# The attention output kept as dimensions by tokens through DRAM, and its sums repeated by the load

## The chip, the core and the metric

The kernel runs on one core of one Trainium2 chip. The metric is the device time of one launch in microseconds (us), the median of several runs. The core has a matrix engine (PE, with its weight loads listed as PEld), a vector engine (DVE), a scalar engine (ACT), a general engine (POOL) and a queue engine (SP) that issues most DMA transfers. DRAM is the chip's large memory, SBUF the one on the core, and PSUM takes what PE writes.

## What is computed

The input x has 4 sequences of 1024 tokens with 256 features, all float32. Three layers follow each other: half a mixture-of-experts layer, attention, and half a mixture-of-experts layer again. The part at issue is the attention and what takes its result in:

```python
def _L0_attn_ref(x, W_dq, W_uq, W_dkv, W_uk, W_uv, W_o):
    ...
    scores = jnp.einsum('bqhd,bkhd->bhqk', Q, K) / math.sqrt(D_K)
    causal = jnp.tril(jnp.ones((Sx, Sx), dtype=bool))
    scores = jnp.where(causal, scores, -jnp.inf)
    attn = jax.nn.softmax(scores, axis=-1)
    out = jnp.einsum('bhqk,bkhd->bqhd', attn, V).reshape(Bx, Sx, N_HEADS * D_K)
    return out @ W_o
...
x = x + 0.5 * _L0_ffn_ref(_layernorm(x, axis=-1), ...)
x = x + _L0_attn_ref(_layernorm(x, axis=-1), ...)
x = x + 0.5 * _L0_ffn_ref(_layernorm(x, axis=-1), ...)
```

There are 16 heads of 16 dimensions, so the attention output of a token has 256 values, and it goes through the 256 by 256 out-projection `W_o`.

## The kernel before

The program is a row of phases, and each ends for all engines before the next begins. Names in the rows carry a short tag of the phase: `a` for the first mixture layer (`al` normalisation and gate scores, `ar` routing, `ae` experts), `q` for the query, key and value projections, `t` for attention, `b` for the second mixture layer (`bl`, `br`, `be`), `s` for the last sum. x stays in SBUF all along, tokens on the partitions, as 32 tiles of 128 tokens (`all_x`).

**Attention** (`phase_attention`) takes 16 groups, each of 4 heads of one sequence. The steps of groups 0 to 2 and 12 to 15 are written out, the nine between them are three passes of a loop over three steps. Step g holds three kinds of PE work, and `plan_step` sets their order by a table of costs:
- the row maxima of groups ahead (`score`, L1320, 48 units a group): PE fills one of three PSUM banks `psR`, DVE takes the maximum out (L1430, L1434). 37 units of the next group and 11 of the one behind it lie in a step, and a small transpose `turn_max` (L1326), whose result SP puts beside the queries by three small DMAs (L1276);
- transposed scores of its own group (`score_t`, L1339, with the causal mask added at L1342), 48 pieces through three banks `psS`, which ACT turns into exponentials (L1410);
- `pv` (L1353): values times exponentials, for 4 heads at once into `psO`, one bank for each half c of 512 query tokens. Rows 32h to 32h+16 of it are the 16 dimensions and, as the 17th, the sum of the exponentials of head h; columns are tokens.

ACT copies each finished `psO` into `oT` (L1398), half 0 some 5 us before half 1, which ends the group. In the next step PE transposes `oT` back to tokens by dimensions (`turn_out`, L1332, four 128 by 128 transposes for each half, at places 4 and 5 of the same three-bank ring), DVE copies the 17 useful columns of each head into `orow` (L1458), and SP stores that, one DMA a half (L1270), to `o_rows` in DRAM, tokens by 16 heads of 17 values. `orow` waits for the store of the group before. On SP the stores of g-1 stand behind the 13 loads of group g+2 (L878, L881) and ahead of the three small DMAs. The last group's two halves are turned after its step, and SP waits for their stores before the phase ends.

**`bl`** (`phase_logits` with `o_dram`) takes the 32 tiles as 8 chunks of four. For a chunk SP loads `raw`, tokens by 272 values (L201); DVE takes the reciprocals of the 64 sums of each partition (L251); POOL multiplies, tile by tile, into `att` (L239); PE transposes `att` twice a tile (`turn_att`, L298), ACT copies the result into `aT` (L348), PE projects (`project`, L290, four matmul instructions a tile, two banks `psW`), DVE adds to x (L258) and takes statistics (L841), then the reciprocal of the deviation (L854) and the normalised rows `xn` (L858), which PE transposes (L307) for the gate scores. In step c of DVE stand the reciprocals of chunk c+2, then the additions and statistics of chunk c, then its `xn`. The step of PE has, for each of four tiles, `project` of c, `turn_att` of c+1 and `turn` of c-1. `project` of a tile waits for the addition of the tile two before it.

## Time and profile before

| | us |
|---|---|
| median of 3 runs | 1361.29 |
| lowest and highest | 1356.99, 1362.87 |
| the profiled execution | 1358.71 |
| its span in the profile | 1356.9 |

| phase | from, to (us of the span) |
|---|---|
| first mixture layer | 0 to 320 |
| projections | 320 to 450 |
| attention | 450 to 992 |
| `bl` | 992 to 1061 |
| rest of the second mixture layer | 1061 to 1317 |
| last sum | 1317 to 1357 |

The engines overlap, so a busy share tells which is nearly always at work but not which one the others wait for. That is read from the waits and, best, from the order of time within one step. A merged line of the timeline stands for several instructions of one kind, from the start of the first, with the length until the end of the last.

### The profile page before, as it was taken

What the parts mean: (1) busy time and instruction counts of PE and PEld (TensorE: products, weight loads), DVE (VectorE), ACT (ScalarE), POOL (GpSimd) and SP (SyncE); (2) the same over time, 40 slices, a digit from 0 to 9 for tenths busy, and PEclk for the clock granted to TensorE, in tenths of its full rate; (3) what the DMA queues carried; (4) which work ended last, traced back from release to release, by engine and by line L of the source; (5) the groups of instructions that cost most, each with busy time, mean ns of one, the idle gap of its engine ahead of it and who ended that gap; (6) DMA issues with size and microseconds to landing.
All of it is one profiled execution on the core that took longest, in us unless ns stands there. A gap on an engine that the chain in (4) does not pass through costs nothing. (4 is left out here: it accounts for less than half of the span.)

```text
span 1356.9 us, 27575 instructions
## 1 busy us (share of the span) xinstructions
PE 1104.6 (81%) x7114; PEld 667.6 (49%) x7117; DVE 853.9 (63%) x2534; ACT 678.2 (50%) x1676; POOL 462.5 (34%) x528
## 2 busy tenths in 40 slices
PE   3538999993885599999999999999869279999960
PEld 2236888772332134344344444444347168878750
DVE  4773444334883788888888788888147744443327
ACT  3513544441564057666666566667636225544430
POOL 3536777671343400000000000000027457777650
PEclk9857999996787589999999999999989659999985
DMA  7701222225656914445545534540046202222239
GB/s 230 223 0 63 94 94 94 94 90 192 209 188 168 168 15 65 67 69 77 74 64 71 76 67 61 81 65 10 10 150 224 78 26 96 93 94 96 85 111 331
DMA packets 130286, 141.06 MB, mean 104 GB/s; under 512 B 46800, under 2 KB 104592, under 8 KB 130192
## 3 DMA queue, kind: packets, MB, share of 16 engines
q1 hardware_dynamic: 112144, 98.04, 32.7%
q0 software_dynamic: 13824, 37.77, 8.2%
q10 hardware_dynamic: 4224, 4.19, 0.9%
q8 instruction: 35, 0.57, 0.2%
q14 instruction: 59, 0.48, 0.1%
HBM read 86.88 MB, written 52.69 MB: 103 GB/s over the span
## 5 line engine op out<-in xcount | busy, mean ns | idle before, releaser
L1410 ACT ACTIVATE t_prob<-t_psS 128x512 f32<-128x512 f32 (+3 forms) x768 | 327.2, 495 | 185.2 <-PE t_psS L1342 150.2
L1430 DVE CUSTOM_DVE_ANT_0 t_psR<-t_psR,all_causal 128x128 f32<-128x128 f32 (+3 forms) x512 | 247.1, 503 | 62.9 <-PE t_psR L1320 53.8
L1320 PE MATMUL t_psR<-stacks_kst,stacks_qst 96*128 96x512 bf16 (+3 forms) x768 | 234.9, 346 | 33.3 <-PEq L888 20.1
L1339 PE MATMUL t_psS<-stacks_qst,stacks_kst 99*128 99x512 bf16 (+3 forms) x768 | 223.7, 332 | 2.4 <-ACT t_prob L1410 1.5
L1434 DVE TENSOR_REDUCE t_maxp<-t_psR 128x1 f32<-128x512 f32 x256 | 175.7, 686 | 21.1 <-PE t_psR L1320 20.8
L1320 PEld LDWEIGHTS t_psR<-stacks_kst,stacks_qst 96*128 96x128 bf16 x768 | 70.1, 98 | 214.3 <-DVE t_maxp L1430 112.4
L1353 PE MATMUL t_psO<-t_prob,t_vst 128*32 128x512 f32 (+3 forms) x1536 | 163.6, 498 | 3.0 <-ACT t_prob L1410 1.1
L1311 POOL COPY t_vst<-stacks_v_rows 128x512 f32<-128x512 f32 x16 | 9.8, 614 | 439.2 <-DMA stacks_v_rows<-v_rows 439.0
L678 PE MATMUL ae_psG<-a_w,ae_xT 128*128 x432 | 116.3, 405 | 3.1 <-DVE ae_xT L765 2.4
L678 PE MATMUL be_psG<-b_w,be_xT 128*128 x432 | 115.7, 403 | 3.0 <-DVE be_xT L765 2.3
L1342 PE MATMUL t_psS<-all_causal_t,all_ident_bf 128*128 128x128 bf16 x512 | 109.6, 221 | 0.0
L776 DVE TENSOR_TENSOR ae_hid<-ae_sg,ae_psG 128x256 f32<-128x256 f32 x72 | 30.3, 421 | 113.7 <-ACT ae_sg L746 110.9
L776 DVE TENSOR_TENSOR be_hid<-be_sg,be_psG 128x256 f32<-128x256 f32 x72 | 30.3, 421 | 113.1 <-ACT be_sg L746 111.6
L1339 PEld LDWEIGHTS t_psS<-stacks_qst,stacks_kst 99*128 99x128 bf16 x768 | 74.1, 98 | 53.7 <-ACT t_prob L1410 29.8
L678 PEld LDWEIGHTS ae_psG<-a_w,ae_xT 128*128 128x128 f32 x432 | 77.2, 191 | 19.1 <-issue 4.7
L678 PEld LDWEIGHTS be_psG<-b_w,be_xT 128*128 128x128 f32 x432 | 76.6, 190 | 18.8 <-issue 4.4
L627 POOL DMA_INDIRECT ae_xg<-xn_rows,ae_index x72 | 70.5, 979 | 32.6 <-issue 13.7
L627 POOL DMA_INDIRECT be_xg<-xn_rows,be_index x72 | 70.3, 976 | 31.9 <-issue 14.6
L634 POOL DMA_INDIRECT y_rows<-be_y,be_target x72 | 70.8, 984 | 24.7 <-issue 17.2
L634 POOL DMA_INDIRECT y_rows<-ae_y,ae_target x72 | 70.8, 983 | 24.7 <-issue 16.9
L1430 DVE DVE_READ_ACCUMULATOR2_ANT t_maxp<- 128x1 f32 x512 | 72.0, 141 | 0.0
L678 PE MATMUL ae_psY<-a_w,ae_hT 128*128 x432 | 68.1, 293 | 0.6 <-ACT ae_y L739 0.6
(289 smaller groups left out, 1899.2 us busy)
## 6 DMA issues: line engine op xcount, KB each, us to landing
qk_parts<-q_parts SPq DMA_DIRECT2D x32, 384.0 KB, 2.6
stacks_qst<-qk_parts SPq DMA_DIRECT2D x96, 128.0 KB, 4.6
stacks_kst<-qk_parts SPq DMA_DIRECT2D x96, 128.0 KB, 7.4
q_yk<-y_rows SPq DMA_DIRECT2D x16, 512.0 KB, 6.3
s_yk<-y_rows SPq DMA_DIRECT2D x16, 512.0 KB, 10.0
o_rows<-t_orow SPq DMA_DIRECT2D x32, 136.0 KB, 8.8
bl_raw<-o_rows SPq DMA_DIRECT2D x8, 544.0 KB, 4.0
xn_rows<-al_xn SPq DMA_DIRECT2D x8, 512.0 KB, 3.8
```

The source lines that it names most:

```text
L627: nc.gpsimd.indirect_dma_start(xg[:, i, :], None, xn_dram, bass.IndirectOffsetOnAxis(ap=index[:, s:s + 1], axis=0)).then_inc(x_loaded[i], 16)
L634: nc.gpsimd.indirect_dma_start(y_dram, bass.IndirectOffsetOnAxis(ap=target[:, s:s + 1], axis=0), y[:, i, :], None).then_inc(y_stored[i], 16)
L678: ins = nc.tensor.matmul(out, lhsT[a][:, s % 2, c, :], W.parts[b][:, c, bass.ds(e, 1), cols].rearrange("p a f -> p (a f)"), start=(n == 0) ...
L776: nc.vector.tensor_tensor(hid[:, s % 2, :], sg[:, s % 2, :], psG[s % 2][:, F:2 * F], ALU.mult).then_inc(hid_ready, 1)
L1311: nc.gpsimd.tensor_copy(heads(vst[k], VW)[:, :, 0:DK], heads(v_rows[k], DK)).then_inc(pool_done, 1)
L1320: nc.tensor.matmul(psR[bank][:, 0:w], qst[slot][0:KROWS, h, i * P:(i + 1) * P], kst[slot][0:KROWS, h, k0:k0 + w], start=True, stop=True).t ...
L1339: ins = nc.tensor.matmul(ps, kst[k][0:MROWS, h, j * P:(j + 1) * P], qst[k][0:MROWS, h, a:(c + 1) * 512], start=True, stop=a > j * P)
L1342: ins = nc.tensor.matmul(ps[:, 0:P], T.ident_bf[:], T.causal_t[:], start=False, stop=True)
L1353: ins = nc.tensor.matmul(psO[c][h * VW:(h + 1) * VW, a - c * 512:512], vst[k][:, j, h * VW:(h + 1) * VW], prob[j % 2][:, h, a:(c + 1) * 51 ...
L1410: nc.scalar.activation(prob[j % 2][:, h, a:(c + 1) * 512], psS[n % ST_BANKS][:, a - c * 512:512], ACT.Exp, scale=DK ** -0.5).then_inc(exp_ ...
L1430: ins = nc.vector.tensor_tensor_reduce(psR[bank][:, 0:w], psR[bank][:, 0:w], T.causal[:, 512 - w:512], 1.0, -BIG, ALU.add, ALU.max, maxp[: ...
L1434: ins = nc.vector.tensor_reduce(maxp[:, h, col:col + 1], psR[bank][:, 0:w], AX_X, ALU.max)
```

## The change

The attention output stays as it leaves `psO`. SP stores `oT` itself into `o_turned`, 16 heads by 17 rows by 4096 tokens: for each half and each of the four heads one DMA of 17 partitions by 512 floats. `turn_out`, `orow` and its copy are gone, so the ring has 49 places a step instead of 51 and `plan_step` lays the step out anew. The copy into `oT` now waits for the stores of the same half of the group before.

In `bl` a chunk is loaded as dimensions by tokens, 2 blocks of 128 dimensions by 512 tokens (`raw`), and beside it `den` of the same shape, in which the load repeats the sum of a head over the 16 partitions of its dimensions: four DMAs of 256 KB. DVE takes the reciprocal of the whole of `den`, in place; POOL multiplies `raw` by `den` into `aT`, 128 by 256 elements for a tile, and PE projects from that. `att`, `psA`, `turn_att` and ACT's copy are gone. The reciprocals of a chunk stand one step ahead of its additions, not two.

```diff
@@ phase_logits, sync
+                tokens = bass.ds(c * (U * P), U * P)
+                for k in range(DC):
+                    heads = slice(k * (P // DK), (k + 1) * (P // DK))
+                    sp.dma_start(raw[:, b, k, :], o_dram[heads, 0:DK, tokens]).then_inc(raw_loaded[b], 16)
+                    sums = bc(o_dram[heads, DK, tokens], 1, [P // DK, DK, U * P])
+                    sp.dma_start(den[:, b, k, :], sums).then_inc(raw_loaded[b], 16)
...
-                if attended and has(4):
-                    hold(sp, att_ready, c * U + (2 * U + U), T)
-                    load(c + 4, b)
+                if attended and has(3) and has(1):
+                    hold(sp, aT_ready, c * U + (U + U), T)
+                    load(c + 3, 1 - b)
@@ gpsimd
+                if attended and has(1):
+                    hold(pool, inv_ready, c + 2, T)
+                    hold(pool, w_done, c * U, T)
                     for s in range(U):
...
+                        nc.gpsimd.tensor_tensor(aT[:, 1 - b, :, tile], raw[:, 1 - b, :, tile], den[:, 1 - b, :, tile],
+                                                ALU.mult).then_inc(aT_ready, 1)
@@ vector
-                if attended and has(2):
-                    dve.wait_ge(raw_loaded[b], (c // 2) * 16 + 32)
-                    wait(dve, att_ready, c * U + U)
-                    nc.vector.reciprocal(inv[:, b], raw[:, b, :, :, DK]).then_inc(inv_ready, 1)
+                if attended and has(1):
+                    dve.wait_ge(raw_loaded[1 - b], ((c + 1) // 2) * (16 * RAW_LOADS) + 16 * RAW_LOADS)
+                    nc.vector.reciprocal(den[:, 1 - b], den[:, 1 - b]).then_inc(inv_ready, 1)
@@ tensor, step
                     if attended and has(0):
-                        project(c, s)
-                    if attended and has(1):
-                        turn_att(c + 1, 1 - b, s)
+                        project(c, b, s)
@@ plan_step
-    if with_before:
-        at = 4 if later else 0
-        ring[at:at] = [("o", c) for c in range(2)]
@@ phase_attention, sync
-                    hold(sp, drained, out_at(g, c), T)
-                    dst = o_dram[bass.ds(b * S + c * 512, 512), bass.ds(hg * (HG * OW), HG * OW)]
-                    sp.dma_start(dst.rearrange("(i p) w -> p i w", p=P),
-                                 orow[:, c].rearrange("p (i h) w -> p i (h w)", h=HG)).then_inc(o_stored[c], 16)
+                    hold(sp, o_copied, g * 2 + c + 1, T)
+                    for h in range(HG):
+                        sp.dma_start(o_dram[bass.ds(hg * HG + h, 1), :, bass.ds(b * S + c * 512, 512)].rearrange("a w t -> (a w) t"),
+                                     oT[h * VW:h * VW + OW, c, :]).then_inc(o_stored[c], 16)
@@ scalar, copy_out
                 act.wait_ge(pv_done, g * PV + n_pv[QHALF * (c + 1) - 1, c] + 1)
+                wait(act, o_stored[c], g * (16 * HG))
                 nc.scalar.copy(oT[:, c, :], psO[c][:]).then_inc(o_copied, 1)
@@ program
-        o_dram = nc.dram_tensor("o_rows", (N, H * OW), F32).ap()
+        o_dram = nc.dram_tensor("o_turned", (H, OW, N), F32).ap()
```

What stands on DVE where `bl` begins, before the change (the last numbers are partitions by elements, and x3 the count of equal instructions in a row):

```order
L251 RECIPROCAL bl_inv<-bl_raw 128x64 x3
L258 TENSOR_TENSOR all_x<-all_x,bl_psW 128x256 x2
L841 BN_STATS bl_stats<-all_x 128x6
L258 TENSOR_TENSOR all_x<-all_x,bl_psW 128x256
L841 BN_STATS bl_stats<-all_x 128x6
```

And after the change:

```order
L252 RECIPROCAL bl_den<-bl_den 128x1024 x2
L259 TENSOR_TENSOR all_x<-all_x,bl_psW 128x256 x2
L826 BN_STATS bl_stats<-all_x 128x6
L259 TENSOR_TENSOR all_x<-all_x,bl_psW 128x256
L826 BN_STATS bl_stats<-all_x 128x6
```

Two reciprocals stand ahead of the first additions instead of three, each over 1024 elements of a partition instead of 64.

PE at the head of the step of group 1, before the change (`t_psR` is the ring of the row maxima, `t_psS` the transposed scores, `t_psO` `pv`):

```order
L1320 MATMUL t_psR<-stacks_kst,stacks_qst 128x384
L1339 MATMUL t_psS<-stacks_qst,stacks_kst 128x512
L1342 MATMUL t_psS<-all_causal_t,all_ident_bf 128x128
L1332 MATMUL t_psR<-all_ident,t_oT 128x128 x8
L1339 MATMUL t_psS<-stacks_qst,stacks_kst 128x512 x2
L1320 MATMUL t_psR<-stacks_kst,stacks_qst 128x512
```

And after it, with the number of each bank kept:

```order
L1292 MATMUL t_psR1<-stacks_kst2,stacks_qst2 128x384
L1304 MATMUL t_psS0<-stacks_qst1,stacks_kst1 128x512
L1307 MATMUL t_psS0<-all_causal_t,all_ident_bf 128x128
L1292 MATMUL t_psR2<-stacks_kst2,stacks_qst2 128x512
L1292 MATMUL t_psR0<-stacks_kst2,stacks_qst2 128x512
L1304 MATMUL t_psS1<-stacks_qst1,stacks_kst1 128x512
```

Two units of row maxima have taken the places of the eight transposes, and the rest of the ring's work has moved up.

## Rows read from the trace of the kernel before

**Rows 1.** Busy time by stretch: us, then PE, PEld, DVE, ACT, POOL, clock, DMA.

```profile
30.00:40.00 10.00, 5.95 (x47) 3.49 (x40) 9.23 (x20) 5.70 (x12) 5.70 (x4) 1.00 0.86 285
60.00:70.00 10.00, 2.58 (x19) 1.08 (x12) 6.67 (x11) 4.68 (x5) 5.61 (x3) 0.50 0.38 113
548.00:900.00 352.00, 341.68 (x2559) 143.35 (x2560) 300.54 (x978) 234.83 (x550) 6.75 (x11) 1.00 0.48 68
990.00:1062.00 72.00, 54.94 (x392) 42.05 (x392) 42.35 (x148) 35.44 (x96) 40.30 (x44) 0.91 0.66 208
1317.00:1357.00 40.00, 0.00 (x0) 0.00 (x0) 25.77 (x64) 0.00 (x0) 0.00 (x0) 0.50 0.93 315
```

**Rows 2.** Timeline of ACT: copies of `psO` of half 1, each ending a group.

```profile
704.87 0.58 ACT L1398 COPY t_oT<-t_psO 128x512 f32<-128x512 f32 x1 [0.55 <-PE t_psO L1353]
...
897.56 0.58 ACT L1398 COPY t_oT<-t_psO 128x512 f32<-128x512 f32 x1 [0.55 <-PE t_psO L1353]
...
928.29 0.58 ACT L1398 COPY t_oT<-t_psO 128x512 f32<-128x512 f32 x1 [0.55 <-PE t_psO L1353]
...
956.73 0.59 ACT L1398 COPY t_oT<-t_psO 128x512 f32<-128x512 f32 x1 [0.55 <-PE t_psO L1353]
```

**Rows 3.** Timeline where a step turns the output of the group before.

```profile
670.91 0.58 ACT L1398 COPY t_oT<-t_psO 128x512 f32<-128x512 f32 x1 [0.55 <-PE t_psO L1353]
...
674.96 0.86 PEld L1332 LDWEIGHTS t_psR<-all_ident,t_oT 128*128 128x128 f32 x8
...
675.76 0.79 DVE L1458 COPY t_orow<-t_psR 128x272 f32<-128x272 f32 x2
675.78 0.21 PEld L1339 LDWEIGHTS t_psS<-stacks_qst,stacks_kst 99*128 99x128 bf16 x2
...
678.13 0.40 SPq L881 DMA_DIRECT2D stacks_v_rows<-v_rows  x1
...
679.53 1.23 SPq L1270 DMA_DIRECT2D o_rows<-t_orow  x2
```

**Rows 4.** Timeline of the last group's start.

```profile
959.51 1.22 PEld L1332 LDWEIGHTS t_psR<-all_ident,t_oT 128*128 128x128 f32 x8 [3.12 <-DMA stacks_qst<-t_mparts]
...
960.71 0.15 PEld L1339 LDWEIGHTS t_psS<-stacks_qst,stacks_kst 99*128 99x128 bf16 x1
```

**Rows 5.** Timeline from the end of attention into `bl`.

```profile
983.48 0.58 ACT L1398 COPY t_oT<-t_psO 128x512 f32<-128x512 f32 x1
...
987.45 0.58 ACT L1398 COPY t_oT<-t_psO 128x512 f32<-128x512 f32 x1 [0.55 <-PE t_psO L1353]
...
988.85 0.44 DVE L1458 COPY t_orow<-t_psR 128x272 f32<-128x272 f32 x1 [0.40 <-PE t_psR L1332]
992.13 0.93 SPq L201 DMA_DIRECT2D bl_raw<-o_rows  x2
995.84 0.55 DVE L251 RECIPROCAL bl_inv<-bl_raw 128x64 f32<-128x64 f32 x1 [6.55 <-DMA bl_raw<-o_rows]
```

**Rows 6.** DMA issues: KB each, median us from issue to landing.

```profile
s_yk<-y_rows SPq DMA_DIRECT2D x16, 512.0 KB, 10.0
o_rows<-t_orow SPq DMA_DIRECT2D x32, 136.0 KB, 8.8
bl_raw<-o_rows SPq DMA_DIRECT2D x8, 544.0 KB, 4.0
stacks_v_rows<-v_rows SPq DMA_DIRECT2D x16, 256.0 KB, 9.3
all_x<-in_x SPq DMA_DIRECT2D x3, 1024.0 KB, 7.5
```

**Rows 7.** The stores of L1270, us from issue to landing, least, median and most.

```profile
L1270 SPq DMA_DIRECT2D o_rows<-t_orow x32: 372/416/712, 519.7 to 989.3; - x32
...
DMA to landing us min/median/max: 2.3/8.8/10.3
```

**Rows 8.** Every reciprocal of the program by line, ns least, median and most.

```profile
L854 DVE RECIPROCAL bl_rstd<-bl_std x8: 177/178/180, 1008.0 to 1055.9; 128x4 f32<-128x4 f32 x8
L478 DVE RECIPROCAL br_gap<-br_den x1: 353/353/353, 1077.7 to 1077.7; 128x32 f32<-128x32 f32 x1
L251 DVE RECIPROCAL bl_inv<-bl_raw x8: 545/548/555, 995.8 to 1037.6; 128x64 f32<-128x64 f32 x8
```

**Rows 9.** Timeline of DVE in `bl`: the first two additions of steps, and the last step.

```profile
1003.02 0.69 DVE L258 TENSOR_TENSOR all_x<-all_x,bl_psW 128x256 f32<-128x256 f32 x2
...
1044.68 0.94 DVE L258 TENSOR_TENSOR all_x<-all_x,bl_psW 128x256 f32<-128x256 f32 x2
...
1051.28 0.93 DVE L258 TENSOR_TENSOR all_x<-all_x,bl_psW 128x256 f32<-128x256 f32 x2
...
1056.14 1.38 DVE L858 TENSOR_SCALAR bl_xn<-all_x,bl_moments,bl_rstd 128x256 f32<-128x256 f32 x4
```

**Rows 10.** Timeline of PE in `bl`: one tile's projection at either clock.

```profile
999.42 1.75 PE L290 MATMUL bl_psW<-all_wo,bl_aT 128*128 128x256 f32 x4
...
1010.47 1.10 PE L290 MATMUL bl_psW<-all_wo,bl_aT 128*128 128x256 f32 x4
```

**Rows 11.** Groups of instructions of `bl` by line.

```profile
L239 POOL TENSOR_TENSOR bl_att<-bl_raw,bl_inv 128x256 f32<-128x256 f32 x32 | 18.8, 620 | 94.3 <-DVE bl_inv L251 89.2 <-PE bl_psA L298 5.0
L298 PE MATMUL bl_psA<-all_ident,bl_att 128*128 128x128 f32 x64 | 13.0, 293 | 8.5 <-POOL bl_att L239 8.4
```

More of the change, by code:

```diff
@@ L162, in phase_logits @@
         CH = NT // U
-        raw, inv = M.sb("raw", [P, 2, U, H, OW]), M.sb("inv", [P, 2, U, H])
-        att = M.sb("att", [P, 2, U, H, DK])
-        aT = M.sb("aT", [P, U, DC, P])
+        raw, den, aT = (M.sb(n, [P, 2, DC, U * P]) for n in ("raw", "den", "aT"))
         xn = M.sb("xn", [P, 2, U, D])
@@ L168, in phase_logits @@
         lT = M.sb("lT", [P, P])
-        psA, psW, psT, psL = ([M.ps(f"{n}{i}", [P, 512]) for i in range(2)] for n in ("psA", "psW", "psT", "psL"))
+        psW, psT, psL = ([M.ps(f"{n}{i}", [P, 512]) for i in range(2)] for n in ("psW", "psT", "psL"))
         xn_stored = [M.sem(f"xn_stored{b}") for b in range(2)]
@@ L289, in project @@
                 for k in range(DC):
[L290 removed]
+                    ins = nc.tensor.matmul(psW[s % 2][:, 0:D], aT[:, b, k, s * P:(s + 1) * P], T.wo[:, k, :], start=(k == 0), stop=(k == DC - 1))
                 ins.then_inc(w_done, 1)
[L293 to L300 removed]
             def turn(c, b, s):
@@ L343, in step @@
                 for s in range(U):
-                    if attended and has(1):
-                        n = (c + 1) * U + s
-                        act.wait_ge(at_done, n + 1)
-                        wait(act, w_done, n + 1 - U)
-                        nc.scalar.copy(aT[:, s], psA[s % 2][:, 0:D].rearrange("p (k t) -> p k t", k=DC)).then_inc(aT_ready, 1)
                     if has(-1):
@@ L1124, in score_units, with plan_step @@
     return units
-def plan_step(units, later, with_before):
+def plan_step(units, later):
     width = lambda j, c: min((c + 1) * 512, S) - max(c * 512, j * P)
@@ L1189, in plan_step @@
             n_pv += 1
-    return order, [x for x in order if x[0] in "smo"]
+    return order, [x for x in order if x[0] in "sm"]
 def phase_attention(nc, T, tag, A, o_dram):
@@ L1276, in load_max, with step @@
                     sp.dma_start(qst[slot][KROWS + part:KROWS + part + 1, :, :], mparts[:, part, :]).then_inc(m_loaded, 16)
-            def step(g, k, later, with_before):
-                if with_before:
+            def step(g, k, later):
+                if not isinstance(g, int) or g:
                     store_out(g - 1)
@@ L1306, in _, with step @@
                 first.link(nc.gpsimd.memset(heads(vst[s], VW)[:, :, DK:DK + 1], 1.0))
-            def step(g, k, later, with_before):
+            def step(g, k, later):
                 hold(pool, loaded[k], ((g - k) // SLOTS) * (16 * N_LOADS) + 16 * N_LOADS, T)
@@ L1356, in pv, with step @@
                 ins.then_inc(pv_done, 1)
-            def step(g, k, later, with_before):
+            def step(g, k, later):
                 base, idx, asked = ring_base(g), 0, False
                 pe.wait_ge(m_loaded, g * (16 * PARTS) + 16 * PARTS)
-                for what, *at in plan_step(units, later, with_before)[0]:
+                for what, *at in plan_step(units, later)[0]:
                     if what == "st":
@@ L1390, in _ @@
             steps(step)(pe)
-            for c in range(2):
-                turn_out(NG - 1, c, out_at(NG - 1, c) - 1, ring_bank(NG - 1, 2 + c))
         @block.scalar
@@ L1453, in split_max, with step @@
                 nc.vector.tensor_tensor(mparts[:, 2], mid[:], mparts[:, 1], ALU.subtract).then_inc(m_ready, 1)
-            def copy_rows(g, c, r, bank):
-                dve.wait_ge(filled, r + 1)
-                wait(dve, o_stored[c], g * 16)
-                nc.vector.tensor_copy(orow[:, c], psR[bank][:].rearrange("p (x w) -> p x w", w=VW)[:, :, 0:OW]).then_inc(drained, 1)
-            def step(g, k, later, with_before):
+            def step(g, k, later):
                 base = ring_base(g)
-                for idx, (what, at, *ahead) in enumerate(plan_step(units, later, with_before)[1]):
-                    r, bank = base + idx, ring_bank(g, idx)
+                for idx, (what, at, *ahead) in enumerate(plan_step(units, later)[1]):
+                    r, bank = base + idx, ring_bank(k, idx)
                     if what == "s":
@@ L1467, in step @@
                             join_max(g + 1, r + 1)
[L1468 removed]
+                    else:
                         split_max(g + 1, r, bank)
[L1470 to L1471 removed]
             for u in range(NS):
@@ L1479, in _ @@
             steps(step)(dve)
-            for c in range(2):
-                copy_rows(NG - 1, c, out_at(NG - 1, c) - 1, ring_bank(NG - 1, 2 + c))
 class Tables:
```

67 lines of the change are left out of this document (16 added, 51 removed).

## The prediction

> **What bounds the kernel now.** I read first the busy time by stretch [rows 1]. Attention is a crowd: over eleven groups PE is busy 97% and DVE 85%, and DMA moves at a 0.48 share. In `bl` PE is busy 54.9 of 72 us, DVE 42.4, POOL 40.3. Neither tells what an instruction there is worth, so I went on to the order of time inside single steps: the copies that end the groups [rows 2], the place where a step turns the group before [rows 3], the hand-over between the phases [rows 5], and the additions of DVE in `bl` [rows 9]. Last I looked for the durations of what the change enlarges: the reciprocal [rows 8] and the DMAs [rows 6, 7].
>
> In attention a full group takes 30.73 us from copy to copy (897.56 to 928.29). The next one, with 11 ring units fewer, takes 28.44 [rows 2]. So ring work has a price in the step, 0.21 us a unit there, and it is not hidden. In `bl` the first additions of successive steps lie 6.60 us apart where PE still transposes `att`, and the last step, without these transposes, is over 6.24 us after its first addition (1051.28 to 1057.52) [rows 9].
>
> **The transposes of the output in attention.** Eight of them hold PE from 674.96 to 675.78, that is 0.82 us, and the two copies hold DVE for 0.79 us [rows 3]. Both engines are nearly full, so I take 0.82 us off each of the steps of groups 1 to 14: 14 x 0.82 = **-11.5**. The bounds: two places of the ring at 0.21 us make 0.42 a step (-5.9), and two places at an even share of a step of 51 places (30.73 / 51 = 0.60) make 1.2 (-16.9). The new order of the step has no row of its own. Its pieces are the same, and I leave what it does to these bounds. The last group begins with the transposes before any other work, from 959.51 to 960.71 [rows 4]: **-1.2**.
>
> **The hand-over.** Now the last copy into `oT` ends at 988.03, two more pieces follow (transposes, a copy that ends at 989.29), the store lands and the first load of `bl` is issued at 992.13 [rows 5]. Afterwards the stores follow `oT` at once, but there are four for the last half. A store issue takes 0.42 us (median) and a quiet 136 KB store landed in 2.3 us [rows 7]: 988.03 + 1.7 + 2.3 is 992.0, no change. That is one end. The other end is that a transfer of 17 partitions runs on one DMA engine. In the last sum the 16 engines moved 315 GB/s at a 0.93 share [rows 1], so one moves 21.2 GB/s, and a store of 34.8 KB takes 1.64 us. Eight of them from 984.1 on (the end of half 0's copy, at 983.48 + 0.58 [rows 5]), plus 1 us to begin and land, end at 998.2: +6.2. The trace has no transfer of such a shape, and I take the middle, **+3**.
>
> On this place a page has a rule. The row shows that a store over 128 partitions runs on several engines, since 136 KB in 2.3 us are 59 GB/s, nearly three times an engine's rate. The Trainium skill, "DMA: Bandwidth & Descriptors", section "Why a DMA increments its semaphore by 16 and not by 1", says that the number of engines is the largest up to 16 that divides the slowest dimension on both sides, and 17 is divided by 1 alone. By that rule the term is +6.2 and the time 3 us more than I forecast.
>
> **The first load of `bl`.** Now 544 KB land 3.7 us after their issue, when DVE starts (992.13 to 995.84) [rows 5]. Afterwards a chunk is 1024 KB in four DMAs. The row of that size is the load of x, 7.5 us [rows 6]: **+3.8**. The lower bound is the three further issues alone, +1.2. The upper one is a landing of 10.0 us, as in the last sum [rows 6], +6.3. The later loads are issued 10 us or more ahead of their use (a chunk's reciprocal and four multiplications make 9.0 us, a whole step 12.7) and I count them as hidden by the longer step.
>
> **The reciprocals.** This is the large term. All reciprocals of the program lie on one line: 178 ns for 4 elements of a partition, 353 for 32, 548 for 64 [rows 8]. That is 175 / 28 = 6.25 and 195 / 32 = 6.1 ns an element. In place of 64 elements, DVE takes 1024: 178 + 1020 x 6.2 = 6.5 us a chunk instead of 0.55. A row has the 64 sums of a partition once; the new layout has each sum 16 times. Nothing hides them, since DVE does them between the `xn` of one chunk and the additions of the next, in the order of its own queue. PE has only two `psW` banks, so behind the reciprocal it can be ahead by two projections and must then wait for the additions. A step becomes the reciprocal plus the rest. For the rest I take the last step's 6.24 us [rows 9], since it is the one step that already has no `turn_att`. From the first landing to the last `xn` that makes 8 x 6.5 + 8 x 6.24 = 101.9 us. Before, it is 1057.52 - 995.84 = 61.7 [rows 5, 9]. The difference is **+40.2**, which has the gain from the transposes in it: 0.36 us a step, for 13.0 us of PE work that is gone [rows 11].
>
> A page bears on this too. The rows give 6.2 ns an element. The Trainium skill, "VectorE: DVE Perf Modes", section "First, the fixed hardware budget", tells that the reciprocal is an iterative divide with a repeat count of 8, where an addition needs one pass; with the engine's 0.96 GHz from "Trainium Kernel Development and Optimization", "NeuronCore Architecture", I estimate 8.3 ns an element, 8.5 us a chunk and some 16 us more in all. The rows differ from that, and the sum goes by them.
>
> **The clock in `bl`.** PE's work there falls from 54.9 to about 42 us while the stretch grows from 72 to some 113, a busy share of 37%. The rows nearest to it are a stretch with PE busy 5.95 of 10 us at the full clock (2.4 GHz) and one with 2.58 of 10 at half of it (1.2 GHz) [rows 1]. A tile's projection takes 1.10 us at the high level and 1.75 at the low one [rows 10]. Two of a step's four projections and a little of the transposes lie on the path, so the low clock costs about 1.6 us a step, 13 in all. Bounds 0 and +13; I take **+4**.
>
> **Edits at nothing.** POOL's multiplication keeps its 128 by 256 elements at 0.62 us [rows 11], four of them hidden by the next reciprocal or the additions; uncovered they would cost 2.5 us a step. ACT's copies into `aT` go from an engine that is not the limit. SP issues six DMAs more a group, 6 x 0.42 = 2.5 us, ahead of the three small DMAs, which wait for a row maximum some 20 us later anyway. The new wait of ACT has behind it the copy and the exponentials of the next group. It is free while the stores of the group before have landed (a rival, below).
>
> **The sum**: -11.5 - 1.2 + 3 + 3.8 + 40.2 + 4 = +38.3. On the profiled execution's own 1358.7 that gives 1397.0. That execution lies 2.6 under the median of the runs, so against 1361.3 it is 1399.6, and I say **1399**. With all ends added, 1361.3 + 23 = 1384 and 1361.3 + 59 = 1420.
>
> **Rival 1: the stores hold ACT.** If each store runs on one engine, eight of them queue there behind the loads of the group. The last of these, issued at 678.13, lands 9.3 us later, at 687.4 [rows 3, 6]. At 1.64 us a store they end at 700.5, and the copy of half 1 comes at 704.87 [rows 2]: no wait. It decides from (704.87 - 687.4) / 8 = 2.2 us a store. In the attention stretch, with many small pieces, an engine moved only 68 / 0.48 / 16 = 8.9 GB/s [rows 1], which would be 3.9 us. Between the two, at 2.6 us, a step is 3.3 us longer, 13 steps make 43, and the hand-over some 10 more: about 1450. For it speaks that rate. Against it speaks that the rate is that of small pieces, and these stores have rows of 2 KB.
>
> **Rival 2, faster: the reciprocal is cheap when long.** If the price fell with length towards that of other float32 operations, 1.4 us for 1024 elements (two additions of 256 take 0.69 [rows 9]), the phase would be 8 x 1.4 + 8 x 6.24 = 61.1 us, 0.6 less than now, the clock would hold, and the sum would be -11.5 - 1.2 + 3 + 3.8 - 0.6 = -6.5: 1355. The sign turns at about 2.2 us a reciprocal. Three sizes on a straight line speak against it.
>
> **Rival 3: the reciprocal is dearer than the line.** Beyond 64 elements there is no row. At 8.5 us each it is 16 us more, 1415.
>
> **Chances.** The forecast 77%, rival 1 10%, rival 2 5%, rival 3 8%. The range has to hold 8 in 10: the forecast's bounds and rival 3 lie in 1384 to 1420, rivals 1 and 2 outside are 15%, and for their near edges I take 1383 to 1426. A measurement of this kernel can tell about 0.5%, or 7 us. Faster by more than that has rival 2's chance, 5%; within it 2%, for a reciprocal priced in between; slower 93%.
>
> **What the profile will show.** Right if the reciprocal on `den` takes 6.5 us with 1024 elements, DVE's first additions in `bl` lie 12.5 to 14 us apart, and PE there waits for `all_x`; if full groups take about 29.9 us instead of 30.73; if DVE starts in `bl` about 14.6 us after the last copy of `psO` ended, where it is 7.8 now (the hand-over's 3 and the load's 3.8 more). Wrong if the reciprocal is far from 6.5, if ACT's copy waits for a DMA in attention, or if a group is not shorter, for then the ring did not limit it. The clock in `bl` tells the last term.

## The result, and where the 65 us lie

| | before | after |
|---|---|---|
| median of the runs, us | 1359.14 (4 runs, 1354.49 to 1362.87) | 1425.85 (4 runs, 1419.86 to 1429.37) |
| profiled execution | 1358.71 | 1424.39 |
| its span | 1356.9 | 1422.3 |

The ratio is 1.048, interval 1.046 to 1.051: slower, by 65.7 us between the profiled executions and by 65.4 between their spans, where the forecast was 38. The median is inside the range given, but only 0.15 us below its upper edge of 1426, and two of the four runs lie above that edge.

The span in pieces, each from one event to the next ("last copy" is the end of ACT's last copy of `psO`):

| piece | before | after | change | forecast |
|---|---|---|---|---|
| start to first exponential of attention | 482.6 | 477.6 | -5.0 | 0 |
| attention, to the last copy | 505.5 | 509.4 | +3.9 | -12.7 |
| hand-over, to the first load of `bl` | 4.1 | 10.3 | +6.2 | +3 |
| first load to first reciprocal | 3.7 | 8.6 | +4.9 | +3.8 |
| first reciprocal to last `xn` | 61.7 | 114.8 | +53.1 | +44.2 |
| rest | 299.4 | 301.8 | +2.4 | 0 |

The first piece holds nothing that the change touches. In further profiles of kernels that leave it alone (of the second session below) it lay between 478.9, for the kernel after again, and 486.5, so its -5.0 is not a gain of the change.

**`bl`.** The timeline of DVE in the kernel after (start us, us, engine, line, operation, what it waited for) begins with two reciprocals in one row; the later rows are one step and the last two steps:

```profile
1005.79 12.96 DVE L252 RECIPROCAL bl_den<-bl_den 128x1024 f32<-128x1024 f32 x2 [49.16 <-DMA bl_den<-o_turned]
1018.67 0.69 DVE L259 TENSOR_TENSOR all_x<-all_x,bl_psW 128x256 f32<-128x256 f32 x2
...
1047.36 0.69 DVE L259 TENSOR_TENSOR all_x<-all_x,bl_psW 128x256 f32 x2
...
1050.06 0.42 DVE L259 TENSOR_TENSOR all_x<-all_x,bl_psW 128x256 f32 x1 [1.68 <-PE bl_psW L291]
...
1055.91 6.55 DVE L252 RECIPROCAL bl_den<-bl_den 128x1024 f32<-128x1024 f32 x1
1062.37 0.69 DVE L259 TENSOR_TENSOR all_x<-all_x,bl_psW 128x256 f32 x2
...
1106.77 0.69 DVE L259 TENSOR_TENSOR all_x<-all_x,bl_psW 128x256 f32<-128x256 f32 x2
...
1114.29 0.93 DVE L259 TENSOR_TENSOR all_x<-all_x,bl_psW 128x256 f32<-128x256 f32 x2
```

The reciprocal takes 6.55 us, and this step 15.01 (1047.36 to 1062.37). The six steps that hold one take 14.1 to 15.0, where the steps of the kernel before took 6.6 to 7.1. Without the reciprocal 8.46 are left of this step, not 6.24. The step at 1106.77, which has no reciprocal any more, takes 7.52, and the last one 6.25 up to the last `xn`. PE shows why. Its timeline beside the same step:

```profile
1062.89 2.04 PE L291 MATMUL bl_psW<-all_wo,bl_aT 128*128 128x256 f32 x4 [6.17 <-DVE all_x L259]
...
1065.15 1.34 PE L291 MATMUL bl_psW<-all_wo,bl_aT 128*128 128x256 f32 x4
```

PE stands 6.17 us for the addition behind the reciprocal, and then a tile's projection takes 2.04 us in place of the 1.10 at the full clock [rows 10]. Busy time by stretch (us, then PE, PEld, DVE, ACT, POOL, granted clock, DMA share, GB/s) for attention, for `bl`, and for two pieces of the step above, the second of them right behind the first:

```profile
478.00:987.00 509.00, 478.15 (x3536) 187.34 (x3533) 391.17 (x1285) 341.23 (x800) 7.98 (x13) 0.97 0.38 58
1006.00:1125.00 119.00, 63.44 (x328) 44.88 (x328) 89.52 (x145) 24.36 (x63) 43.80 (x44) 0.73 0.44 146
1059.00:1065.80 6.80, 2.91 (x8) 2.39 (x9) 5.13 (x6) 0.37 (x1) 3.20 (x5) 0.50 0.36 124
1066.00:1076.00 10.00, 4.07 (x34) 2.70 (x32) 8.62 (x13) 2.97 (x7) 3.58 (x2) 1.00 0.67 227
```

In `bl` the mean granted clock is 0.73, where [rows 1] shows 0.91. Within the step it goes down to its lower level (0.50) while PE waits, and is back at the upper one (1.00) 3 us after PE has begun again.

**The hand-over.** SP's timeline in the kernel after:

```profile
987.01 1.38 SPq L1242 DMA_DIRECT2D o_turned<-t_oT  x4
997.23 0.73 SPq L201 DMA_DIRECT2D bl_raw<-o_turned  x1
```

The four stores are issued by 988.4, and the first load follows 8.8 us later. In [rows 5] it was issued 2.8 us after DVE's last copy. The same view as above, for a stretch in which nothing but these stores moves, and for one in which nothing but the first loads of `bl` does:

```profile
989.00:996.00 7.00, 0.00 (x0) 0.00 (x0) 0.00 (x0) 0.00 (x0) 0.00 (x0) 0.50 0.07 26
1000.00:1006.00 6.00, 0.00 (x0) 0.00 (x0) 0.21 (x1) 0.00 (x0) 0.00 (x0) 0.50 0.52 188
```

One engine of 16 would be a share of 0.06, eight would be 0.50. So the eight stores of 17 partitions share one DMA engine, at 26 GB/s, and the loads run on eight.

**Attention.** Copies of `psO` of half 1 in the kernel after, as in [rows 2] (timeline of ACT):

```profile
663.05 0.58 ACT L1360 COPY t_oT<-t_psO 128x512 f32<-128x512 f32 x1 [0.54 <-PE t_psO L1318]
...
703.85 0.58 ACT L1360 COPY t_oT<-t_psO 128x512 f32<-128x512 f32 x1 [0.55 <-PE t_psO L1318]
...
898.64 0.58 ACT L1360 COPY t_oT<-t_psO 128x512 f32<-128x512 f32 x1 [0.55 <-PE t_psO L1318]
...
929.17 0.58 ACT L1360 COPY t_oT<-t_psO 128x512 f32<-128x512 f32 x1 [0.54 <-PE t_psO L1318]
...
956.98 0.58 ACT L1360 COPY t_oT<-t_psO 128x512 f32<-128x512 f32 x1 [0.54 <-PE t_psO L1318]
```

A full written-out group takes 30.53 us (898.64 to 929.17) where it took 30.73, the next 27.81 for 28.44. In the loop a group went from 31.6 to 30.9. All steps but two together gained 8.9 us; 1.3 of them are the last group, which no longer begins with the transposes (the forecast's -1.2). The two others are those in which the loop turns back to its start. One stands above: 703.85 - 663.05 = 40.80, before 34.0; the other is 40.9, before 35.6. That is +12.1, and the start of attention up to the first copy has the last +0.7. The timeline of such a turn-back in the kernel after, PE's rows:

```profile
662.56 0.43 PE L1318 MATMUL t_psO<-t_prob,t_vst 128*32 128x128 f32 x8 [0.37 <-ACT t_prob L1372]
666.49 0.61 PE L1292 MATMUL t_psR<-stacks_kst,stacks_qst 96*128 96x512 bf16 x1 [3.50 <-issue]
...
667.53 0.63 PE L1304 MATMUL t_psS<-stacks_qst,stacks_kst 99*128 99x512 bf16 x1
671.36 0.29 PE L1307 MATMUL t_psS<-all_causal_t,all_ident_bf 128*128 128x128 bf16 x1 [3.19 <-issue]
```

PE waits twice for "issue", that is for nothing that another engine or a transfer gives, 3.50 and 3.19 us, and behind them its matmuls run at the low clock for a while. The summary of PE's waits in attention has these first; in the kernel before the same operation has 0.4 us of it (the last row):

```profile
PE t_psR L1292 <- issue: 7.5, 2, 4.0
PE t_psS L1307 <- issue: 6.1, 2, 3.2
```

```profile
PE t_psR L1320 <- issue: 0.4, 2, 0.2
```

What makes the turn-back of the kernel before longer than its other steps is of another kind. PE waits there for a row maximum of DVE:

```profile
674.56 0.34 PE L1320 MATMUL t_psR<-stacks_kst,stacks_qst 96*128 96x384 bf16 x1 [2.15 <-DVE t_maxp L1430]
```

The page's table of DMA queues has two rows for queues that bring instructions. One, q14, is the same in both kernels (58 and 59 packets). The other is not. After, then before:

```profile
q8 instruction: 52, 0.85, 0.3%
```

```profile
q8 instruction: 35, 0.57, 0.2%
```

The same table for the second and third pass of the loop alone shows where they come. The kernel after, 663 to 870 us:

```profile
q8 instruction: 18, 0.29, 0.6%
```

The kernel before, 671 to 870 us, has no row of q8 at all, only the other instruction queue:

```profile
q14 instruction: 24, 0.20, 0.4%
```

If q8 is PE's own queue, as its packets suggest, then in the kernel before the code that the first pass brought serves the other two, and in the kernel after it is brought again in each pass, nine packets a pass.

### The profile page after: what moved, and what is told of

Read it like the earlier page. It is cut to its first block and busy times, and to the rows that moved or that the text cites. A ratio compares the mean times of both kernels' runs of the same rounds, so it can differ in the third digit from the quotient of the medians.

```text
span 1422.3 us, 27208 instructions
## 1 busy us (share of the span) xinstructions
PE 1100.5 (77%) x6924; PEld 654.9 (46%) x6925; DVE 887.3 (62%) x2502; ACT 668.0 (47%) x1644; POOL 465.9 (33%) x528
## 5 line engine op out<-in xcount | busy, mean ns | idle before, releaser
L1292 PE MATMUL t_psR<-stacks_kst,stacks_qst 96*128 96x512 bf16 (+3 forms) x768 | 242.5, 348 | 37.3 <-PEq L873 20.1
L1304 PE MATMUL t_psS<-stacks_qst,stacks_kst 99*128 99x512 bf16 (+3 forms) x768 | 228.3, 337 | 5.3 <-DMA stacks_qst<-t_mparts 2.8
L291 PE MATMUL bl_psW<-all_wo,bl_aT 128*128 128x256 f32 x128 | 47.9, 517 | 66.0 <-DVE all_x L259 39.1
L252 DVE RECIPROCAL bl_den<-bl_den 128x1024 f32<-128x1024 f32 x8 | 52.3, 6543 | 49.2 <-DMA bl_den<-o_turned 49.2
L619 POOL DMA_INDIRECT y_rows<-ae_y,ae_target x72 | 70.8, 984 | 24.7 <-issue 16.6
## 6 DMA issues: line engine op xcount, KB each, us to landing
s_yk<-y_rows SPq DMA_DIRECT2D x16, 512.0 KB, 10.1
```

Of the source, the lines that this page charges most:

```text
L252: nc.vector.reciprocal(den[:, 1 - b], den[:, 1 - b]).then_inc(inv_ready, 1)
L619: nc.gpsimd.indirect_dma_start(y_dram, bass.IndirectOffsetOnAxis(ap=target[:, s:s + 1], axis=0), y[:, i, :], None).then_inc(y_stored[i], 16)
L1292: nc.tensor.matmul(psR[bank][:, 0:w], qst[slot][0:KROWS, h, i * P:(i + 1) * P], kst[slot][0:KROWS, h, k0:k0 + w], start=True, stop=True).t ...
L1304: ins = nc.tensor.matmul(ps, kst[k][0:MROWS, h, j * P:(j + 1) * P], qst[k][0:MROWS, h, a:(c + 1) * 512], start=True, stop=a > j * P)
```

## The experiments

**The theories.** A: the hand-over is long because a store of 17 partitions runs on one DMA engine. For the turn-backs B: the stores, all on one engine, crowd the transfers that bring PE's code; C: they depend on where PE's loop code lies. For `bl`: the reciprocal and, through PE's waits behind it, the clock.

The first four kernels ran in a session in which the kernel before took 1422.93 us (median of 7 runs). Its phases ahead of attention and behind `bl` were longer there, by the profiles of these four (509 to 517 us to the first exponential in place of 478), while attention and `bl` took what they take elsewhere. So these four are read by their ratio to that and by their pieces. In the session of the next four the kernel before took 1362.13, in that of the last 1359.49.

### spread: stores of 16 partitions

The four sums of a half go out in a fifth transfer.

```diff
+                    tokens = bass.ds(b * S + c * 512, 512)
                     for h in range(HG):
-                        sp.dma_start(o_dram[bass.ds(hg * HG + h, 1), :, bass.ds(b * S + c * 512, 512)].rearrange("a w t -> (a w) t"),
-                                     oT[h * VW:h * VW + OW, c, :]).then_inc(o_stored[c], 16)
+                        sp.dma_start(o_dram[bass.ds(hg * HG + h, 1), 0:DK, tokens].rearrange("a w t -> (a w) t"),
+                                     oT[h * VW:h * VW + DK, c, :]).then_inc(o_stored[c], 16)
+                    sp.dma_start(o_dram[bass.ds(hg * HG, HG), DK, tokens], oT[DK:P:VW, c, :]).then_inc(o_stored[c], 16)
...
```

> The changed kernel with one part altered: the 16 rows of a head go out in a DMA of 16 partitions, and the four sums of a half in a fifth DMA, in place of four DMAs of 17 partitions. Theory A (a transfer of 17 partitions runs on one DMA engine): the time from the end of the last copy of psO (10.2 us before the first load of bl now) falls to about 5, SP no longer spends 6 to 9 us on issuing the eight stores of a group, 1425.9 becomes about 1420. On the two steps of attention that take 40.8 us in place of 30.8 there are two theories. Theory B (the stores crowd the DMA engine that also brings code): they fall to about 34 as before the change, 14 us less in all, 1406. Theory C (where PE's code lies against the pieces in which it is fetched): PE's code is the same in this kernel, so they stay near 40.8 and the time is about 1420.

Measured: 1482.83 us, ratio 1.040 (1.035 to 1.045). Attention 508.2, turn-backs 40.1 and 40.9, `bl` 114.6. The hand-over is 3.98 in place of 10.3. ACT's last copy and SP:

```profile
1024.49 0.58 ACT L1362 COPY t_oT<-t_psO 128x512 f32<-128x512 f32 x1 [0.55 <-PE t_psO L1320]
```

```profile
1025.10 1.71 SPq L1243 DMA_DIRECT2D o_turned<-t_oT  x4
1026.85 0.52 SPq L1245 DMA_DIRECT2D o_turned<-t_oT  x1
1029.05 0.70 SPq L201 DMA_DIRECT2D bl_raw<-o_turned  x1
```

The same bytes, in more transfers, let the first load go 6.3 us earlier, because a transfer has 16 partitions and not 17. With the DMA share of 0.07 above, A stands. The turn-backs do not move, so B falls.

### pad: sixteen small matmuls ahead of PE's first group

```diff
+            for _ in range(16):
+                nc.tensor.matmul(psS[0][:, 0:P], T.ident_bf[:], T.causal_t[:], start=True, stop=True)
             pe.wait_ge(loaded[0], 16 * N_LOADS)
```

> The changed kernel with 16 small matmuls more at the start of PE's attention phase, where PE waits for loads anyway; they write a bank that is overwritten before its first use. Nothing else changes but the place of all later PE code. Theory C (the place of the code makes the stalls of 3.8, 3.8 and 1.4 us at the loop's two turns back): the steps of 40.8 us change, to 35 to 37 where one of the stalls is gone, 8 to 12 us less in all, 1414 to 1418. Theory B (the stores crowd the DMA engine that brings code): no change, 1425.

Measured: 1482.81 us, ratio 1.041 (1.037 to 1.045). The turn-backs take 36.1 and 34.6 us, attention 499.2 where the kernel after has 509.4; every other step is unchanged to 0.1 us, but for the last group, 0.4 longer. PE's waits in attention and the instruction queue:

```profile
PE t_psR L1292 <- issue: 0.4, 2, 0.2
```

```profile
q8 instruction: 34, 0.56, 0.2%
```

Adding work to PE took 10 us away. The 18 packets of the loop's second and third pass are gone too: from 700 to 907 us, those two passes, the table again has no row of q8. C stands.

### short_recip: the reciprocal over 64 elements

The reciprocal leaves out all but the first 64 of the 1024 elements of a partition.

```diff
-                    nc.vector.reciprocal(den[:, 1 - b], den[:, 1 - b]).then_inc(inv_ready, 1)
+                    nc.vector.reciprocal(den[:, 1 - b, 0, 0:64], den[:, 1 - b, 0, 0:64]).then_inc(inv_ready, 1)
```

> The changed kernel with DVE's reciprocal over 64 elements of a partition in place of 1024; the other sums are multiplied with as they are, so this part of the computation is left out. Forecast's theory: eight times 6.0 us go, and the granted clock in bl goes back to 0.95 or more, which gives 12 us more: 1425.9 becomes about 1366, and bl from the first reciprocal to the last xn takes 52 to 56 us in place of 114.8. Rival (the rest of a step is long for another reason, the four loads of 1 MB a chunk or POOL): only the 48 us go, the steps stay at 7.9 us, 1378.

Measured: 1449.59 us, ratio 1.018 (1.014 to 1.022). From the first reciprocal to the last `xn` 72.0 us, 42.8 less than after, but 10 more than before and far from the expectation. Two steps take 6.3 and 6.9 us, the next four 10.0 to 10.2. The rival on record, steps of 7.9, missed too. The granted clock is 0.91 (1041 to 1114). DVE's timeline:

```profile
1053.78 0.55 DVE L252 RECIPROCAL bl_den<-bl_den 128x64 f32<-128x64 f32 x1
1060.68 0.55 DVE L252 RECIPROCAL bl_den<-bl_den 128x64 f32<-128x64 f32 x1 [0.26 <-DMA bl_den<-o_turned]
1070.72 0.55 DVE L252 RECIPROCAL bl_den<-bl_den 128x64 f32<-128x64 f32 x1 [2.92 <-DMA bl_den<-o_turned]
1080.67 0.55 DVE L252 RECIPROCAL bl_den<-bl_den 128x64 f32<-128x64 f32 x1 [1.33 <-DMA bl_den<-o_turned]
```

The loads are the next limit. The transfers of a chunk in a step are 1024 KB of `raw` and `den`, 512 KB of `xn` and 768 KB of expert weights. The first megabyte runs on 8 engines (the share of 0.52 above), one for each head of the slowest dimension. If the rest is cut over 16, which is an assumption here, the busiest engine has 128 + 80 = 208 KB a step, at 21.2 GB/s (the rate of an engine, as in the prediction) 10.0 us. That is the measured step. The Trainium skill ("DMA: Bandwidth & Descriptors", "Why a DMA increments its semaphore by 16 and not by 1") gives the number of engines as the largest up to 16 that divides the slowest dimension on both sides; that is 8 here and 1 for the 17 partitions of the stores. The trace agrees with both, by the shares 0.52 and 0.07.

### warm: idle matmuls where PE waits in `bl`

```diff
...
+                    if attended and has(0) and has(1) and s == 1:
+                        for _ in range(5):
+                            nc.tensor.matmul(psF[:], T.ident[:], T.causal[:], start=True, stop=True)
```

> The changed kernel with five idle matmuls (float32, 512 columns, into a bank that nobody reads) on PE in each step of bl that has a reciprocal, placed where PE waits for DVE. Clock theory: the clock stays up in bl (0.73 now), the part of a step behind the reciprocal falls from about 8.0 to 6.3 us, seven steps make 12 us, 1414. Rival (the clock is not what makes these steps long): the step stays at 14.5 us or grows by the idle matmuls, 1426 or more.

Measured: 1478.38 us, ratio 1.039 (1.035 to 1.044). `bl` takes 105.4 us instead of 114.8. The first two steps, in which the clock is still low in part (0.80 from 1036 to 1064), take 13.9 and 14.3 us, the other four that have a reciprocal 13.0, where the kernel after has 14.4 to 15.0:

```profile
1090.24 0.68 DVE L260 TENSOR_TENSOR all_x<-all_x,bl_psW 128x256 f32 x2
...
1096.76 6.54 DVE L253 RECIPROCAL bl_den<-bl_den 128x1024 f32<-128x1024 f32 x1
1103.22 0.68 DVE L260 TENSOR_TENSOR all_x<-all_x,bl_psW 128x256 f32 x2
```

The stretch 1036 to 1140 has a clock of 0.93. 12.98 - 6.54 leaves 6.44, close to the 6.24 that the prediction took for the rest of a step. So 9.4 of the 12.7 us that the steps are longer than forecast are the clock. Most of the rest lies in those first two steps.

### after_again and spread_pad: both repairs at once

> The changed kernel as it is, measured beside the kernel before on the chip of the other experiments. It gives the number that they are read against. Expected: 63 to 67 us over the kernel before; hand-over (last copy of psO to first load of the out-projection) 10.2 us; attention 509 with the two turn-backs at 40.8 and 40.9; first reciprocal to last normalised tile 114.8 us.

Measured: 1427.23 us (4 runs), ratio 1.049 (1.045 to 1.053). Hand-over 10.2, `bl` 114.4, turn-backs 39.4 and 39.1, 1.4 and 1.8 us less than in the first profile. So the price of a long turn-back moves by 2 us or so from one execution to the next.

> Both edits at once: stores of 16 partitions with one transfer for the sums of a half, and sixteen small matmuls ahead of PE's first attention group, which move the place of PE's loop code. If the hand-over (one DMA engine) and the turn-back (place of the code) are independent, both gains are had: hand-over near 4.0, turn-backs near 35, about 16 us less than the changed kernel. If the turn-back instead depends on how the whole of the instruction traffic falls in time, its gain need not come back: turn-backs anywhere from 35 to 41, 6 to 16 us less.

Measured: 1413.25 us, ratio 1.037 (1.033 to 1.042), 14.0 less than the kernel after in the same session. Hand-over 3.99 (-6.2), turn-backs 36.0 and 34.6 (-7.8 together): 14.0. The two gains add. That the sum of the pieces meets the difference of the medians to 0.1 us is chance, since each set of runs spreads over some 8 us.

### before_pad: the same sixteen matmuls in the kernel before

> The kernel before with the same sixteen small matmuls ahead of PE's first attention group. Before, the two turn-backs take 34.0 and 35.6 us in place of 31.6. Theory C (what a turn-back costs depends on where the loop's code lies, by chance of the layout): the two pitches change, by up to 7 us each way, and the other pitches stay at 30.7 to 32.5. Rival: they cost what they cost because of what the other engines' shorter attention loop leaves uncovered, and in the kernel before the cover is there: both stay within 1 us.

Measured: 1360.78 us (10 runs), ratio 1.0005 (0.998 to 1.003). The turn-backs are 34.1 and 35.6, as without them, and the instruction queue has 35 packets, as before. The forecast from C for this kernel missed, and the rival on record came true in its number, both within 1 us. Its reason was that the other engines cover the turn-back here. That cannot be the cause of the long turn-backs, since `pad` removed them with the other engines as they were. What goes with the long turn-back is the count of instruction packets: 52 with 38 to 41 us (the kernel after in both its profiles, `spread`, `warm`, `short_recip`), 34 or 35 with 33 to 36 (before, `before_pad`, and all with the sixteen matmuls). So the layout doesn't shift the price gradually. There are two levels: either the loop's second and third pass bring no code, or they bring all of it again. This kernel is on the lower one with the matmuls and without, and its turn-backs, longer than its other steps by DVE's row maximum, have nothing to lose. The Trainium skill ("Runtime: NRT & Kernel Launch", "Instruction fetch mechanics") says that instructions come in blocks of 16 KiB, ahead of time only in sequence, and that a taken branch out of the blocks that are held stalls until its target is fetched. The rows agree: 17 packets more and 0.28 MB more are 16 KB each, and the stalls lie at the branch. The packets of the second and third pass, 18 in the kernel after and none in the kernel before or in `pad`, show the rest of it in this case. Which block the loop has too many, and how far the code would have to move to bring it back, no run placed.

### compact: the idea without its prices

The sums are kept apart as rows of their own, the reciprocals are taken on them with 64 numbers a partition and chunk, stored again, and the repeating load brings reciprocals. Partitions are ordered by dimension first, so that a load's slowest dimension is 16, stores are those of `spread`, and the sixteen matmuls are in. The core of the diff:

```diff
+        self.dims = nc.dram_tensor("o_dims", (DC, DK, 8, N), F32).ap()
+        self.sums = nc.dram_tensor("o_sums", (DC, 8, N), F32).ap()
+        self.inv = nc.dram_tensor("o_inv", (DC, 8, N), F32).ap()
...
+                    sp.dma_start(raw[:, b, k, :], o_dram.dims[k, :, :, tokens].rearrange("d h t -> (d h) t")).then_inc(raw_loaded[b], 16)
+                    inv = bc(o_dram.inv[k, :, tokens], 0, [DK, 8, U * P])
+                    sp.dma_start(den[:, b, k, :], inv).then_inc(raw_loaded[b], 16)
...
-                    nc.vector.reciprocal(den[:, 1 - b], den[:, 1 - b]).then_inc(inv_ready, 1)
...
+            nc.vector.reciprocal(sums[:], sums[:]).then_inc(inv_ready, 1)
```

> The idea of the change with its three prices taken out. The attention output is stored in 16-partition pieces, the sums apart as rows of their own; the reciprocals are taken over 64 numbers a partition in place of 1024 (six chunks in attention's last step, two at the start of the out-projection), stored, and the repeating load brings the reciprocals; each load spans 128 rows that lie apart, so that it should be cut over all 16 DMA engines; the sixteen small matmuls are in. Computed is all of the reference. Theory (the added time is the hand-over, the turn-backs, the repeated reciprocals and what they leave of the clock): attention 498 to 502, hand-over 4 to 5, first load to first work 5 to 8 because of the two small transfers with the reciprocals between them, steps of the out-projection 6.0 to 7.5, so 50 to 56 in all: 5 to 15 us less than the kernel before. Rival, that the loads bound it as in the run with the short reciprocals: steps of 10, 72 in all, 8 to 15 us more than the kernel before. Rival, that the code's new place brings the turn-backs back: attention 509, no difference from the kernel before to 5 us less.

Measured: 1360.93 us (10 runs), ratio 1.002 (0.999 to 1.005), no difference from the kernel before. Yet its pieces came out nearly as expected: attention 496.8 (turn-backs 34.8 and 34.6), hand-over 4.0, 7.4 us from the first load to POOL's first multiplication, steps in `bl` 6.1 to 8.5 (56.3 in all, expected 50 to 56). The loads have the same bytes as in `short_recip`, and with 16 as the slowest dimension the steps of 10 us are gone. From the last copy to the last `xn` it is 72.3 us, before 69.5. The rest was lost where nothing was expected. SP's timeline in the first layer:

```profile
57.29 10.07 SPq L1579 DMA_DIRECT2D all_wo<-in_w_o  x16
67.40 0.58 SPq L225 DMA_DIRECT2D xn_rows<-al_xn  x1
```

The rows of `W_o` had to be put in the new order, which I did with sixteen transfers. Their issues hold SP for 10.07 us, ahead of a store that routing waits for, and the first router starts at 71.5 where it starts at 62.9 before.

### compact2: four transfers, behind the last step

```diff
-        weights += [(T.wo[q:P:8, k, :], W_o[((q // 2) * 4 + 2 * k + q % 2) * DK:((q // 2) * 4 + 2 * k + q % 2 + 1) * DK, :]) for k in range(DC) for q in range(8)]
+        wo_view = W_o.rearrange("(g k j d) n -> k j d g n", g=4, k=DC, j=2)
+        weights += [(T.wo[j:P:2, k, :], wo_view[k, j]) for k in range(DC) for j in range(2)]
```

> As the compact version, but the out-projection's weight, whose rows stand in the new order, comes in by four transfers in place of sixteen, and SP issues them behind the first layer's last step and not ahead of two stores. In the compact version these sixteen took SP 10.07 us (57.29 to 67.36) and moved the first router's start from 62.9 to 71.5. Theory (the compact version's gain of attention, 8.7 us, was given back there): the first router starts at 62 to 64 again, attention, hand-over and out-projection as in the compact version, so 7 to 9 us less than it, 0.5 to 0.7% below the kernel before. Rival, that the gain was lost elsewhere (phases ahead of the attention vary between 477 and 487 by themselves): within 3 us of the compact version.

Measured: 1353.92 us (12 runs), before 1359.49 (17 runs), ratio 0.9956 (0.9938 to 0.9974). It is faster than both kernels, than the one before by 0.4%, which is small but outside the interval of the runs. SP's timeline, first layer and start of `bl`, and POOL's first multiplications in `bl`:

```profile
60.67 2.50 SPq L1582 DMA_DIRECT2D all_wo<-in_w_o  x4
```

```profile
981.63 0.38 SPq L215 DMA_DIRECT2D bl_raw<-o_dims  x1
```

```profile
988.58 2.77 POOL L261 TENSOR_TENSOR bl_aT<-bl_raw,bl_den 128x256 f32<-128x256 f32 x4 [84.38 <-DMA bl_den<-o_inv]
```

The router starts at 63.9. Attention takes 497.6 (7.8 less than before). From the last copy to the last `xn` it is 74.7, 5.2 more than before. One part is that the first megabyte takes 7 us to land. The other is the last two steps, 10.1 and 8.2 us:

```profile
1038.89 5.30 DVE L863 TENSOR_SCALAR bl_xn<-all_x,bl_moments,bl_rstd 128x256 f32<-128x256 f32 x4
...
1040.37 3.67 POOL L164 TENSOR_TENSOR b_w<-b_w 128x768 fp32r<-128x768 f32 x2
...
1044.66 2.05 PE L311 MATMUL bl_psW<-all_wo,bl_aT 128*128 128x256 f32 x4 [3.15 <-DVE all_x L279]
```

```profile
1034.00:1044.00 10.00, 6.22 (x45) 4.36 (x43) 8.62 (x18) 4.05 (x11) 9.97 (x8) 0.98 0.59 210
1044.00:1052.30 8.30, 6.29 (x33) 4.30 (x33) 4.93 (x18) 2.63 (x6) 0.19 (x2) 0.62 0.54 161
```

The step of 10.1 still has the full clock (0.98). In it DVE's four `xn` operations take 5.30 us, where they take 1.4 to 2.2 in its other steps, and meanwhile POOL prepares expert weights (L164). In the kernel before no `xn` of `bl` runs beside POOL's weight work, and the longest single one takes 415 ns; here the longest takes 1898. In `compact` it is 1890, in its two steps of 8.5. That the two engines hinder each other there is the likely reading; no run separated them. PE then waits 3.15 us, and the last step runs at a mean clock of 0.62. These pieces are what a next version would have to go for.

## The prediction, step by step

Direction and largest term were right. That the number fell inside the range is luck: it lies 0.15 us below the edge, and of the signs named beforehand three came out otherwise. The steps of `bl` are 14.1 to 15.0 us and not 12.5 to 14, a written-out group takes 30.5 and not 29.9, and DVE starts in `bl` 18.8 us after the last copy and not 14.6.

**The reciprocals: right.** 6.55 us for 1024 elements against 6.5 from the straight line through three small sizes [rows 8]. Eight make 52.3 us, forecast 52. Rival 2 (cheap when long) and rival 3 (8.5 us) did not happen. Nor did rival 1: in the summary of ACT's waits the copies into `oT` wait for PE alone (8.7 us in 16 times). That nothing hides the reciprocal holds too: DVE's rows have it between `xn` and the additions, and PE waits 39.1 us for `all_x` in seven steps.

**The clock in `bl`: mis-sized.** I set +4 between 0 and +13. The parts of the steps outside the reciprocal add up to 62.6 us instead of 8 x 6.24 = 49.9, so the term is +12.7. With `warm`, 9.4 of it went away. I took a third of the bound and had no row for that choice. The step had the reason in it: behind a wait of 6.2 us, in every step, the clock is at its lower level and a tile's projection takes 2.04 us. The bound was itself too low for that, since it priced such a projection at 1.75.

**The hand-over: mis-sized.** +6.2, the upper end. The middle was no case of its own: either 17 partitions run on one engine or they do not, and one of the two had to be chosen. `spread` and the DMA share of 0.07 show that they do. That end took 21.2 GB/s for an engine that moved 26; its +6.2 fits all the same. **The first load**: +4.9 for +3.8, within its bounds; 1024 KB over 8 engines at 21.2 GB/s are 6.2 us, and with the 2.3 us for the landing of a quiet store [rows 7] 8.5, measured 8.6. The forecast did not have the eight engines in it, and came close without them.

**Attention: the step that failed.** I multiplied 0.82 us by 14 equal steps. What the steps have in common gained 0.2 us where they are written out and 0.7 in the loop, 8.9 us in 13 steps, so "about 29.9 instead of 30.73" was wrong (30.53). That PE was free for 0.82 us more did not shorten a written-out step by as much. Why these gained less than those in the loop was not tried. What the sum lacked altogether was the two steps at which the loop turns back. They were in the trace of before, 34.0 and 35.6 us among steps of 31.6, but what made them long there was DVE's row maximum, so asking would not have given the price. They grew by 12.1 us, because the loop's new code no longer stays in place from pass to pass. `pad` took 8 us (in `spread_pad`) to 10 of them away without touching the change.

By the table above, attention is 16.6 us over the forecast, `bl` 8.9, the hand-over 3.2, the load 1.1. The untouched pieces give 2.6 back. That makes the 27 us between forecast and profile. The sign and the mechanism of the largest term were right. The error lies in side costs, all of them on the same side.

## What to carry to other kernels

Before DMA repeats data so that it lies well, ask which engine then works on the repeated data: the reciprocal of 64 numbers became one of 1024, and the 9 us that the layout gained in attention's common steps stood against 53 there. Moved to where the numbers stand once, and with its other prices taken out, the same layout wins, by 0.4%. Look at the slowest dimension of every transfer: 17 ran on one engine here and 8 on eight, and with 16 both prices were gone. Count each further DMA on its queue at 0.4 to 0.6 us. When a loop is changed, compare the step at its turn-back apart from the others, and look at the packets of the instruction queues in its later passes. None means that its code stays; here the change of code between the kernels brought 18 and 12 us, and sixteen small matmuls took them away again.

## What the runs showed of the hardware

- A loop's turn-back can cost PE stalls of 2.9 to 4.0 us, two in a row. The loop's later passes then bring their code again, 9 packets of 16 KB each; in the kernel before and in `pad` they bring none. Sixteen more matmuls ahead of the loop removed the stalls in one kernel and changed nothing in another, which had none.
- Transfers of 34 KB with 17 partitions run on one DMA engine, at 26 GB/s, and make the hand-over 10.3 us; with 16 partitions it is 4.0.
- SP's issue of a store of 17 partitions has a median of 366 ns, but takes up to 4308 ns (the row of line L1242 below); of 16 partitions, in `spread`, up to 1486. That the issue itself waits for the one engine is the likely reading.
- DVE's reciprocal stays on one line from 4 to 1024 elements of a partition, at 6.2 ns an element.

```profile
L1242 SPq DMA_DIRECT2D o_turned<-t_oT x128: 225/366/4308, 515.4 to 988.1; - x128
```
